# The norms ahead of a second cross attention and of the last experts by token halves, with the sums before them kept by halves

## The reference

```python
x = x + _L0_xattn_ref(_layernorm(x), ctx_512, ...)   # norm 0, stage A
x = x + _L0_attn_ref(_layernorm(x), ...)             # norm 1, stage B
x = x + _L0_ffn_ref(_layernorm(x), ...)              # norm 2, stage C: two passes over 8 experts
x = x + _L1_xattn_ref(_layernorm(x), ctx_512, ...)   # norm 3, stage D
x = x + _L1_attn_ref(_layernorm(x), ...)             # norm 4, stage E: state space mixer
x = x + _L1_ffn_ref(_layernorm(x), ...)              # norm 5, stage F: 8 gated experts
...
def _layernorm(x, axis=-1, eps=1e-05):
    m = jnp.mean(x, axis=axis, keepdims=True)
    v = jnp.var(x, axis=axis, keepdims=True)
    return (x - m) / jnp.sqrt(v + eps)
```

## Time and profile before

| what | value |
|---|---|
| median of 3 runs | 1344.7 us (1341.34 to 1345.23) |
| the profiled execution's own time | 1340.9 us |
| its span | 1339.1 us |
| TensorE busy | 1312.5 us (98%), 8554 matmuls |
| VectorE, GpSimd, ScalarE busy | 891.6, 650.5, 633.0 us |
| mean granted clock of TensorE | 0.999 |

### The profile page before, as it was taken

How to read it: one execution, slowest core, us unless ns; L and a number is a source line. 1 busy time by engine, 2 the same in 40 slices (tenths; PEclk the granted TensorE clock), 3 DMA queues, 4 the chain that set the end, 5 groups by cost and what they waited for, 6 DMA issues and landing times.

```text
span 1339.1 us, 22014 instructions
## 1 busy us (share of the span) xinstructions
PE 1312.5 (98%) x8554; PEld 1078.6 (81%) x8560; DVE 891.6 (67%) x1413; ACT 633.0 (47%) x1307; POOL 650.5 (49%) x478
## 2 busy tenths in 40 slices
PE   8999999999999998999999999999999999999999
PEld 5777778778876665999999999999878888767887
DVE  5556776659668887777777777777447777564222
ACT  3524443353334435666666666666325446632111
POOL 3343477768746756153153252300565656535664
PEclk9999999999999999999999999999999999999999
DMA  4121223323334220000000001000231221312222
GB/s 153 50 79 49 56 81 94 93 78 87 94 115 137 73 61 33 1 26 26 1 27 26 1 26 38 21 1 5 74 110 49 78 80 64 95 40 88 94 94 79
DMA packets 31619, 83.16 MB, mean 62 GB/s; under 512 B 3489, under 2 KB 5665, under 8 KB 31265
## 3 DMA queue, kind: packets, MB, share of 16 engines
q1 hardware_dynamic: 31520, 81.81, 19.6%
HBM read 80.75 MB, written 1.05 MB: 61 GB/s over the span
## 4 chain that ended last, share of the span: by engine, by line
PE 91%; DVE 4%; ACT 3%; issue 1%; POOL 0%; POOLq 0%; DVEq 0%
PE psum L930 24%; PE psum L931 23%; PE psum L932 23%; PE psum L1482 6%; PE psum L958 1%; PE psum L1416 1%; PE psum L1000 1%; PE psum L1429 1%; PE psum L1005 1%; PE psum L1001 1%; PE psum L1378 1%; PE psum L969 1%; PE psum L1685 1%; DVE xc L2275 1%; PE psum L1659 1%
## 5 line engine op out<-in xcount | busy, mean ns | idle before, releaser
L672 POOL TENSOR_SCALAR wpair<-landing 128x1024 fp32r<-128x1024 f32 (+3 forms) x115 | 98.3, 855 | 373.6 <-PE psum L932 220.1
L930 PE MATMUL psum<-xn,wpair 128*128 128x512 f32 x548 | 222.0, 405 | 0.4 <-POOL wpair L675 0.4
L675 POOL TENSOR_TENSOR wpair<-landing,wpair 128x1024 fp32r<-128x1024 f32 (+3 forms) x115 | 216.2, 1880 | 9.6
L931 PE MATMUL psum<-xn,wpair 128*128 128x512 f32 x548 | 215.6, 393 | 0.0
L932 PE MATMUL psum<-xn,wpair 128*128 128x512 f32 x548 | 215.5, 393 | 0.0
L2268 DVE TENSOR_TENSOR expo_t<-psum,expo_t 128x512 fp32r<-128x512 f32 (+1 forms) x224 | 144.5, 651 | 74.8 <-ACT expo_t L2042 71.2
L2042 ACT CAST expo_t<-psum 128x512 fp32r<-128x512 f32 (+1 forms) x224 | 124.3, 565 | 115.5 <-PE psum L1482 115.5
L930 PE MATMUL psum<-expo_t,kv_pair 128*128 128x256 f32 (+1 forms) x416 | 133.5, 321 | 0.2 <-DVE expo_t L2268 0.2
L1482 PE MATMUL psum<-const,expo 128*128 128x128 f32 (+1 forms) x832 | 127.6, 273 | 0.9 <-DVE expo_t L2268 0.7
L930 PEld LDWEIGHTS psum<-xn,wpair 128*128 128x128 f32 x548 | 102.9, 188 | 30.6 <-issue 7.0
L778 POOL TENSOR_TENSOR wpair<-landing,wpair 128x512 fp32r<-128x512 f32 x80 | 121.0, 1512 | 6.7
(11 more groups left out here) (328 smaller groups left out, 3008.2 us busy)
## 6 DMA issues: line engine op xcount, KB each, us to landing
landing<-in_weights SPq DMA_DIRECT2D x60, 512.0 KB, 3.3
landing<-in_weights SPq DMA_DIRECT2D x103, 256.0 KB, 2.6
kv<-in_ctx SPq DMA_DIRECT2D x8, 832.0 KB, 4.5
landing<-in_weights SPq DMA_DIRECT2D x15, 320.0 KB, 2.9
landing<-in_weights SPq DMA_DIRECT2D x16, 192.0 KB, 2.4
rotary_w<-in_rotary SPq DMA_DIRECT2D x1, 1920.0 KB, 7.8
rope_k<-in_rope_k SPq DMA_DIRECT2D x1, 1664.0 KB, 11.4
const<-in_constants SPq DMA_DIRECT2D x1, 1184.0 KB, 8.4
```

The costliest lines, as they stand in the source:

```text
L672: pool.tensor_scalar(wpair[:, slot, 0, 0:width], landing[:, slot, 0:width], 1.0, 1.0, ALU.mult, ALU.mult).then_inc(chunk_high, 1)
L675: pool.tensor_tensor(wpair[:, slot, 1, 0:width], landing[:, slot, 0:width], wpair[:, slot, 0, 0:width].bitcast(F32), ALU.subtract).then_in ...
L930: pe.matmul(out, w(0), act(0), start=start, stop=False)
L931: pe.matmul(out, w(0), act(1), start=False, stop=False)
```

## The change

In the second expert pass each sum bank holds two feature tiles of one half of the tokens in place of one tile of all tokens, so each matmul of 512 columns becomes two of 256, and bias rows too. The output sums of stage E are kept in the same way. Norms 3 and 5 take half 0 through mean, centre, squares and square sum before half 1. The last down products and the last output chunk are ordered by halves. Half 1's square sums move behind the first three groups of matmuls, ScalarE makes its squares (VectorE did), and the matmuls on zeros go. In stage D both state tiles run in all five groups. In stage F the tiles of banks 2 and 3 are cut into halves and two of the four quarters stand around half 1's square sums, and `turn_logits` stands behind the third. `y_sum` goes: banks are scaled in place. Squares of stage E are made up to one chunk earlier.

```diff
@@ TensorE, last expert of the second pass (before: down_products(p, NE - 1, 3))
+            def last_down_by_halves():
+                e = NE - 1
+                n = c_chunks(1, e)[1]
...
+                down_tile(e, 0, 0)
+                down_tile(e, 1, 0).then_inc(mixed_out, 1)
+                chunk_ready(n + 1)
+                down_tile(e, 2, 0)
+                down_tile(e, 3, 0).then_inc(mixed_out, 1)
+                down_tile(e, 0, 1)
+                down_tile(e, 1, 1).then_inc(chunk_used, 1)
+                half_means(3, 0)
+                down_tile(e, 2, 1)
+                down_tile(e, 3, 1).then_inc(chunk_used, 1)
+                for pair in range(2):
+                    half_square_sums(3, 0, pair)
+                half_means(3, 1)
@@ the sums of the other experts, and of output chunks alike
+            def down_tile(e, m, half):
+                n = c_chunks(1, e)[1]
+                for k in range(2):
+                    mm = product(sums_tile(half, m), quarter_tile(n + m // 2, 2 * (m % 2) + k),
+                                 lambda part: mid_pairs[:, e % 2, part, k, HALVES[half]],
+                                 stop=e == NE - 1 and k == 1 and m % 2 == 1)
+                return mm
@@ TensorE, stage D
-                layer_norm(3, 2)
...
-                normal_tiles(3, [(bank(0), slot_tile(DB % 2, 0), chunk_used)],
-                             [(bank(6), slot_tile((DB + 1) % 2, 0), chunk_used)])
+                for group in range(3):
+                    normal_group(3, group, [*first_states, *second_states])
+                for pair in range(2):
+                    half_square_sums(3, 1, pair)
+                for group in (3, 4):
+                    normal_group(3, group, [*first_states, *second_states])
@@ TensorE, last output chunk and stage F
+                output_half(0, (0, 1)).then_inc(e_out, 1)
+                output_half(0, (2, 3)).then_inc(e_out, 1)
+                output_half(1, (0, 1)).then_inc(e_out, 1)
+                half_means(5, 0)
+                output_half(1, (2, 3)).then_inc(chunk_used, 1)
+                for pair in range(2):
+                    half_square_sums(5, 0, pair)
+                half_means(5, 1)
...
+                normal_group(5, 0, opening)
+                normal_group(5, 1, opening)
+                normal_group(5, 2, opening)
                 chunk_ready(FB + 1)
-                wide((FB + 1) % 2, 0, xn, bank(2)).then_inc(second, 1)
+                second_half_tile(0, 0)
+                for pair in range(2):
+                    half_square_sums(5, 1, pair)
+                second_half_tile(1, 0)
+                normal_group(5, 3, opening)
+                normal_group(5, 4, opening)
+                second_half_tile(0, 1).then_inc(second, 1)
                 turn_logits(2)
-                wide((FB + 1) % 2, FT, xn, bank(3)).then_inc(chunk_used, 1)
+                second_half_tile(1, 1).then_inc(chunk_used, 1)
@@ ScalarE, a norm by halves
+                if k in HALF_BANKS:
+                    deviation(0)
+                    for group in range(3):
+                        high(group)
+                    late_squares(0)
+                    late_squares(1)
+                    deviation(1)
+                    high(3)
+                    high(4)
+                    return
@@ VectorE, a norm by halves (added: sums_added of stage C, outputs_added of stage E)
+            def layer_norm_by_halves(k, added):
+                dve.wait_ge(ln_mean, MEANS_BEFORE[k] + 1)
+                centre(k, 0, bank(HALF_BANKS[k][0])[:, 0:T // 2])
+                added(3)
+                normalise(k, 0)
+                normalise(k, 1)
+                normal_low(k, 0)
+                normalise(k, 2)
+                normal_low(k, 1)
+                dve.wait_ge(ln_mean, MEANS_BEFORE[k] + 2)
+                centre(k, 1, bank(HALF_BANKS[k][1])[:, 0:T // 2])
+                normal_low(k, 2)
+                normalise(k, 3)
+                normalise(k, 4)
+                normal_low(k, 3)
+                normal_low(k, 4)
@@ VectorE, sums of stage E into x (b = half and pair of tiles)
-                    dve.tensor_tensor(y_sum[:, m % 2, :], bank(m), rstd[:, :], ALU.mult).then_inc(e_scaled, 1)
+                    scaled = bank(b).rearrange("p (m t) -> p m t", m=2)
+                    dve.tensor_tensor(scaled, scaled, rstd[:, HALVES[half]].unsqueeze(1).broadcast_to([P, 2, T // 2]), ALU.mult
+                                      ).then_inc(e_scaled, 1)
+                    dve.wait_ge(e_scaled, b + 1)
+                    tiles = x[:, 2 * pair:2 * pair + 2, HALVES[half]]
+                    dve.tensor_tensor(tiles, tiles, scaled, ALU.add).then_inc(x_ready, 1)
```

More of the change, by code:

```diff
@@ L990, in half_tokens, with half_means @@
                 return lambda part: xn[:, part, f, HALVES[half]]
-            def normal_tiles(k, tiles, later=()):
[L994 to L1008, removed]
+            def half_means(k, half):
+                for pair in range(2):
+                    pe.wait_ge(x_ready, 4 * (k - 1) + 2 * half + pair + 1)
+                    for f in (2 * pair, 2 * pair + 1):
+                        mm = pe.matmul(bank(HALF_BANKS[k][half])[:, 0:T // 2], mean_w[:, :], x[:, f, HALVES[half]],
+                                       start=f == 0, stop=f == FT - 1)
+                mm.then_inc(ln_mean, 1)
@@ new lines, in half_square_sums @@
+            def half_square_sums(k, half, pair):
+                if half:
+                    pe.wait_ge(ln_squared_late, 2 * (k - 1) + pair + 1)
+                else:
+                    pe.wait_ge(ln_squared, 2 * k + 2 + pair + 1)
+                for f in (2 * pair, 2 * pair + 1):
+                    mm = pe.matmul(bank(HALF_BANKS[k][2 + half])[:, 0:T // 2], mean_w[:, :], sq[:, f, HALVES[half]],
+                                   start=f == 0, stop=f == FT - 1)
+                if pair:
+                    mm.then_inc(ln_var, 1)
@@ new lines, in half_tiles, with normal_group @@
+            def half_tiles(half, m):
+                return bank(2 * half + m // 2)[:, (m % 2) * (T // 2):(m % 2 + 1) * (T // 2)]
+            def normal_group(k, group, tiles):
+                half, first_f, end_f = NORMAL_GROUPS[group]
+                pe.wait_ge(ln_high, 5 * k + group + 1)
+                for out, weights_of, _ in tiles:
+                    for f in range(first_f, end_f):
+                        w, act = weights_of(f), half_tokens(half, f)
+                        pe.matmul(out[:, HALVES[half]], w(0), act(0), start=f == 0, stop=False)
+                        pe.matmul(out[:, HALVES[half]], w(1), act(0), start=False, stop=False)
+                pe.wait_ge(ln_low, 5 * k + group + 1)
+                for out, weights_of, signal in tiles:
+                    for f in range(first_f, end_f):
+                        mm = pe.matmul(out[:, HALVES[half]], weights_of(f)(0), half_tokens(half, f)(1),
+                                       start=False, stop=f == FT - 1)
+                    if half and end_f == FT:
+                        mm.then_inc(signal, 1)
@@ L1009, in normal_tiles @@
+            def normal_tiles(k, tiles, later=()):
+                for group, (half, _, _) in enumerate(NORMAL_GROUPS):
+                    normal_group(k, group, tiles if half else [*tiles, *later])
                 for out, weights_of, signal in later:
@@ L1714, in output_chunk, with output_half @@
                         for m in range(FT):
[L1715 to L1721, removed]
-                    mm.then_inc(chunk_used, 1)
+                            for half in range(2):
+                                mm = output_tile(c, kk, m, half)
+                    mm.then_inc(chunk_used, 1)
+                def output_half(half, tiles):
+                    for m in tiles:
+                        for kk in range(2):
+                            mm = output_tile(7, kk, m, half)
+                    return mm
                 output_chunk(0)
@@ L1787, in _, with variances @@
         def _(act):
+            def variances(k, half):
+                return bank(HALF_BANKS[k][2 + half] if k in HALF_BANKS else LN_BANKS[k][1 + half])[:, 0:T // 2]
             def layer_norm(k):
```

172 lines of the change are left out of this document (104 added, 68 removed).

## The result

| | median | range | runs |
|---|---|---|---|
| before | 1343.2 us | 1340.9 to 1345.5 | 8 |
| changed | 1348.3 us | 1346.4 to 1350.0 | 8 |

The ratio is 1.0033, with a 95% interval of 1.0021 to 1.0046. By the medians the change costs 5.0 us (by the ratio 4.4, interval 2.8 to 6.2) where 5.7 were forecast, so it is slower, as the walk said. The median itself was forecast at 1350.4; of the 2.1 us between that and 1348.3, 1.5 come from the kernel before, whose median of 8 runs is 1343.2 and not 1344.7. The parts of the sum did not come out alike, though, and that is what the experiments are about.

What follows compares the result with a forecast made beforehand. TensorE, busy 98% of the span, was taken to bound the kernel. Terms of 2.3 + 2.9 + 0.45 = +5.7 us on a median of 1344.7 gave 1350.4 us, range 1343 to 1355.

Steps and rivals of the forecast that it cites:

- the walk: Step-by-step predicted timeline through norms 3 and 5 by halves; with the split's cost it gave +5.7 us; chance 0.45.
- The bound: Whole kernel: TensorE, busy 98% of the span at full clock, sets the time, so work it gains counts in full.
- Part 1: Second expert pass and output chunks: 336 matmuls become pairs of halves, 0.0069 us a pair, +2.3 us.
- the price of 0.120: Assumed spacing in us of 256-column matmuls, from eleven spacings at 404.07 to 405.39 us, used for the halved sums.
- Part 2: Norm 3 to the head: half 1's uncovered chain ends state tiles later and head's chunk is freed later, +2.9 us.
- rival (d): Clock falls without zeros in norm 3's 2.7 us idle; groups 3 and 4 take 2.9 more, +8.6 us; chance 0.07.
- "The zeros that go cost nothing": Norm 3: removing the matmuls on zeros costs 0, since they fill the wait and do not make it.
- Part 3: Norm 5 and routing: halves gain about 0.6 us, the routing's shorter cover takes it back; +0.45 us in all.
- Part 4: Stage E's earlier squares and the removed `y_sum`: no wait found there before, same VectorE sizes, 0.
- (a): Same time: split matmuls cost nothing, or norm 3's second chain is shorter; sum +3.4 or +2.7 us; chance 0.30.
- (b): Faster: halves hide both norms' waits nearly entirely, -4.1 us, 1340.6; chance 0.10.
- (c): Much slower: 256 columns too short to hide the weight load, +56 us, chance 0.02; milder form +12.9, chance 0.06.

Runs made afterwards that it cites:

- experiment 3: Changed kernel plus ten matmuls on zeros between norm 3's second square sums and group 3 of the state tiles; 1343.4 us, ratio 1.0011.
- experiment 4: Kernel before without its six matmuls on zeros ahead of the square sums of norms 3 and 5; 1342.6 us, ratio 1.0000.
- experiment 6: Changed kernel with `turn_logits(2)` six matmuls earlier, inside stage F's third quarter tile; 1345.6 us, ratio 1.0020.
- `norm5_only`: The change in stages E and F alone, with stages C and D as in the kernel before; 1344.3 us, ratio 1.0012.
- `before_no_zeros`: Same run as experiment 4: kernel before without the matmuls on zeros in norms 3 and 5; 1342.6 us, ratio 1.0000.
- `cover_d`: Changed kernel with the second state tile's half 0 behind norm 3's second square sums and its half 1 at the end; 1343.6 us, ratio 1.0007.
- `tuned_d`: Change in stages C and D only, square sums behind group 1, group 2 beside their chain, second tile's half 1 last; 1343.9 us, ratio 1.0007.
- `spread_dt`: Kernel before with stage E's 32 small matmuls laid in four groups between full-size matmuls; 1344.9 us, ratio 1.0017.
- `tuned_f`: Change in stages E and F only, more work behind norm 5's second square sums, routing asked earlier, square means ahead of chunk 6; 1340.8 us, ratio 0.9986.
- experiment 1: The change in stages C and D alone, with norm 5 and output sums as in the kernel before; 1345.3 us, ratio 1.0025.
- experiment 7: Changed kernel with stage E's output sums cut again, into matmuls of 128 columns; 1386.6 us, ratio 1.0331.

## Why the prediction came out as it did

**The bound** held: by the stretches, waits and clock on TensorE made the time.

**Part 1, forecast +2.3, measured +0.55: mis-sized.** In the second pass the last expert starts 85.56 us behind the pass's first bias matmul (385.74 - 300.18), before it was 85.53 (384.42 - 298.89): 168 pairs cost nothing, at 0.117 a half. In stage E 168 pairs cost 0.55 us, 3.3 ns each. The step that failed is the price of 0.120: it came from state tiles, another stream than the sums it was used for. The eleven spacings were no accident of a norm's end nearby: matmuls on `xn` run at 0.120 in longer streams without a wait too, as in the kernel before behind norm 4, 19 spacings in 2.27 us:

```profile
1008.55 0.28 PE L1000 MATMUL psum<-xn,wpair 128*128 128x256 f32 x1
...
1010.82 0.28 PE L1001 MATMUL psum<-xn,wpair 128*128 128x256 f32 x1
```

With the same shape, the halves of `mid_pairs` go at 0.117, those of `decay_in` at 0.118 and those of `xn` at 0.120; why they differ is open. The lower bound, 0, was the right one for the expert sums. The estimate after the Trainium skill ("TensorE: Matmul & The Clock Gate", Back-to-back issue gap) was 0.8 us for 336 pairs; measured was 0.55, in one place 0 and in the other 3.3 ns a pair where the rule has 2.5. Its absolute figures the trace does not bear out for these fp32r matmuls: a half takes 0.117 us, against 262 cycles, 0.109 at 2.4 GHz.

**Part 2, forecast +2.9, measured +4.10: the walk right, and a rival on top of it.** The last expert starts 1.32 us later in the trace than in the walk (launch 1.29). With that added, the walk had half 0's square sums at 393.54, the first products at 397.54, half 1's square sums at 401.2, group 3 at 405.6 and the head at 410.3; the trace has 393.28, 397.28, 400.96, 405.24 and 411.46. Up to group 3 the walk is 0.4 us too long over 20 us. At full clock the part cost 2.60 (experiment 3). The other 1.50 is rival (d), which I gave 0.07. Its mechanism was right and its price, 2.9, too high. It put all 24 matmuls of groups 3 and 4 at half clock, 0.12 us dearer each. The fall, from 405.7 to 409.1, took in 16 of them and made each 0.0925 dearer (0.2125 against 0.12), 1.48 us. It is over before the wait for the head's split begins. "The zeros that go cost nothing" is thus the sentence that failed, though not as a statement on the old zeros: the old order loses nothing without them (experiment 4), the new one loses 1.5 us.

**Part 3, forecast +0.45, measured +0.60.** Norm 5 +1.25, routing -0.65. Its waits of 0.76, 0.96 and 1.37 us are the walk's 0.5, 1.2 and 1.7. The claim that the shorter cover of the routing eats the gain is borne out by experiment 6.

**Part 4, forecast 0:** nothing to be seen in either trace, in no stretch is 0.1 us left for it.

**The sum.** By the stretches the change costs 2.60 + 0.55 + 0.60 = 3.75 us at full clock and 1.50 of clock behind norm 3, together 5.3 against 5.0 by the medians (and 3.75 against 3.2 at equal clock). The forecast of 5.7 was close partly by luck: 1.75 too much in part 1 stood against 1.5 of clock that was not in the sum. The fall in stage E that adds 1.53 to the trace after is not the change's: eight of the eleven experiments show it too, `norm5_only` and `before_no_zeros` among them, whose programs are the old one up to there or but for zeros; it is missing in `cover_d` and `tuned_d`, at that place in `spread_dt`, and in the trace before. What makes the +1.29 ahead of the first expert, in a part that the change does not touch, is open; the traces scatter by 2.4 us there.

**Rivals.** (a) had part 1 right for stage C and was near with its +3.4 at full clock. (b) is refuted for the change as made, as half 1's chain stays bare; `tuned_f`, which puts work beside that chain of norm 5, loses the wait of 0.96 us there and comes out 1.3 under the kernel before, though its other two moves have a share in that (0.7 from the routing). In stage D I had found no such work, and there was some: group 2 and half a tile. It pays back the loss and no more. (c) fell: a half takes 0.117.

**The clock, what is shown and what is not.** A fall at norm 3 is in four of four traces with the wait ahead of group 3 left empty, 2.39 us in each (the changed kernel and experiments 1, 6 and 7). It begins between 0.3 us before the end of that wait and 0.6 behind it. In none of the nine others does the clock fall there: neither with zeros in the wait, nor with 12 matmuls, nor with the old order with or without zeros. So at norm 3 the empty wait calls it. How long a wait is does not settle it in general. All traces have a wait of 1.8 to 2.1 us near 22 us, and in nine of them, both kernels of the result among them, the clock falls between 0.1 us before its end and 1.5 behind it; in the other four it does not. In the kernel before:

```profile
21.68 0.39 PE L1000 MATMUL psum<-xn,wpair 128*128 128x256 f32 x1 [1.79 <-ACT v_tok L1830]
```

```profile
23.00:26.60 3.60, 3.02 (x16) 2.73 (x14) 0.74 (x5) 0.54 (x1) 0.39 (x1) 0.53 0.28 73
```

The first row of the table is 160.6 to 162.1 us long in those nine and 159.7 to 159.9 in the four. And one of the twelve runs of `spread_dt` has a mean clock of 1.000, so it had no fall in spite of the same program.

What calls the falls in stage E is open. In all nine traces that have one (the changed kernel's and those of eight experiments) it begins 3.0 to 4.3 us behind the start of the 32 small matmuls, which is why they remain the suspect; but four traces have no fall there, three of them with the same row of small matmuls. How often runs fall also differs between kernels in a way that nothing here explains: a mean clock of 0.997 or less is in 47 of 87 runs of the kernel before, in 1 of 12 of `cover_d` and in 8 of 12 of `tuned_d`.

## What to carry to other kernels

Take the price of a split matmul from the spacing of starts, not from durations, and don't carry it from one stream to another within a few ns, even at the same shape: 0.120 against 0.117 made 1.8 us of this sum. A norm by halves saves nothing if the second half's chain has no work beside it: keep back whole tiles for it before ordering the rest. If a new wait of some microseconds opens on TensorE ahead of dense work, fill it, if only with zeros, and look at the granted clock in windows of a few microseconds, as the page's slices don't show a fall of 3.4 us.

## What I had not expected of the hardware

With full 128x128 weights, matmuls of 512, 256 and 128 columns started 0.233, 0.117 to 0.118 and 0.112 us apart, so that halving 512 is nearly free and halving 256 nearly doubles the time. A fall of the clock at a 2.4 us empty wait lasted 3.4 us and cost 1.5 us, in the stretch behind the wait. And in stage E of the changed kernel the clock fell though TensorE had no idle time ahead of it. TensorE's timeline of the changed kernel there:

```profile
1016.73 3.78 PE L1705 MATMUL psum<-small,xc 128*128 128x32 f32 x32
1020.32 0.77 PE L933 MATMUL psum<-xn,wpair 128*128 128x512 f32 x1
...
1021.74 0.63 PE L933 MATMUL psum<-xn,wpair 128*128 128x512 f32 x1
1022.17 0.63 PE L934 MATMUL psum<-xn,wpair 128*128 128x512 f32 x1
```

Behind 32 matmuls of 32 columns, recorded without a gap, those of 512 columns start 0.43 us apart in place of 0.233: the clock is at 1.2 GHz.
